# Causal attention on one core: TensorE takes the pieces of the weighted sum before a step's transposes

## The reference

```
q, k, v = x @ w_aq, x @ w_ak, x @ w_av         # 8 heads of 128
q, k = rope(q), rope(k)                        # rotary embedding
s = q k^T / 128, causal mask; p = softmax(s)   # 1024 x 1024 a head
r = sum over heads of (p v) @ w_ao
x = layernorm(x + r)
x = layernorm(x + ffn(x))                      # 128 -> 512 -> 512 -> 512 -> 128
```

## Time and profile before

| what | value |
|---|---|
| median of 3 runs | 1065.4 us (1064.43 to 1065.68) |
| profiled execution | 1065.99 us |
| its span, first to last instruction | 1064.2 us |
| attention stage, by the trace | from the start to about 773 us |
| mean granted TensorE clock | 0.981 of full speed |

### The profile page before, as it was taken

One profiled execution on the slowest core, in us unless ns is written; L12 is line 12 of the kernel. 1 busy time (PEld: TensorE's weight loads), 2 busy tenths in 40 slices (PEclk: granted clock), 3 DMA queues, 4 the chain that ended last, 5 costly groups with the idle time before them and its releaser, 6 DMA issues. The chain is left out here.

```text
span 1064.2 us, 19686 instructions
## 1 busy us (share of the span) xinstructions
PE 997.1 (94%) x5648; PEld 860.2 (81%) x5648; DVE 820.6 (77%) x1803; ACT 593.3 (56%) x1255; POOL 539.6 (51%) x536
## 2 busy tenths in 40 slices
PE   3799999999999999999999999999839999999995
PEld 3688888898888889888888888888728878788784
DVE  5888888888888888887888888788555677486744
ACT  3566666665666666566666666666434252433521
POOL 4666767776676776677677666767250101000000
PEclk9899999999999999999999999999969999999998
DMA  8433233432322123323222222221020000000000
GB/s 282 150 127 74 61 80 97 124 99 56 75 69 69 49 59 100 70 61 79 59 49 59 61 70 68 72 59 40 1 80 1 1 1 21 1 20 0 1 20 21
DMA packets 33292, 66.16 MB, mean 62 GB/s; under 512 B 5457, under 2 KB 6993, under 8 KB 32209
## 3 DMA queue, kind: packets, MB, share of 16 engines
q1 hardware_dynamic: 30400, 58.62, 21.0%
q10 hardware_dynamic: 2832, 6.82, 1.7%
HBM read 24.26 MB, written 7.34 MB: 30 GB/s over the span
## 5 line engine op out<-in xcount | busy, mean ns | idle before, releaser
L703 POOL TENSOR_SCALAR probs<-probs,inv_sum 128x128 f32<-128x128 f32 (+7 forms) x256 | 191.1, 747 | 232.4 <-DVE inv_sum L621 231.8
L534 ACT ACTIVATE pT<-psum 128x512 fp32r<-128x512 f32 (+3 forms) x384 | 173.9, 490 | 144.0 <-PE psum L401 141.9
L308 PE MATMUL psum<-pT,vals 128*128 128x512 f32 (+3 forms) x1152 | 242.6, 351 | 1.6 <-DVE rT L663 1.6
L522 ACT ACTIVATE probs<-psum,neg_max 128x128 f32<-128x128 f32 (+7 forms) x256 | 190.5, 744 | 80.2 <-DVE neg_max L615 79.8
L615 DVE TENSOR_REDUCE neg_max<-psum 128x1 f32<-128x128 f32 (+7 forms) x256 | 191.2, 747 | 54.8 <-PE psum L392 53.6
L631 DVE TENSOR_TENSOR pT<-psum,pT 128x512 fp32r<-128x512 f32 (+3 forms) x384 | 200.7, 551 | 32.3 <-ACT pT L534 25.3
L308 PEld LDWEIGHTS psum<-pT,vals 128*128 128x128 f32 x1152 | 187.7, 189 | 23.9 <-DVE pT L631 1.7
L401 PE MATMUL psum<-ident,probs 128*128 128x128 f32 x1152 | 173.7, 277 | 12.9 <-POOL probs L703 12.2
L883 PE MATMUL ps<-hid,w 128*128 128x512 f32 x768 | 181.3, 396 | 0.0
L708 POOL TENSOR_TENSOR swapped<-by_cos,swapped 128x512 f32<-128x512 f32 x128 | 164.7, 1298 | 14.2 <-DMA swapped<-by_sin 14.2
L883 PEld LDWEIGHTS ps<-hid,w 128*128 128x128 f32 x768 | 143.7, 188 | 34.5
(11 more groups left out here) (77 smaller groups left out, 1195.3 us busy)
## 6 DMA issues: line engine op xcount, KB each, us to landing
swapped<-by_sin SPq DMA_DIRECT2D x256, 128.0 KB, 2.3
w_stage<-qk_split SPq DMA_DIRECT2D x30, 256.0 KB, 2.7
wv_stage<-v_split SPq DMA_DIRECT2D x15, 256.0 KB, 2.7
x_split<-ffn_raw ACTq DMA_DIRECT2D x2, 1024.0 KB, 5.8
ffn_raw<-g SPq DMA_DIRECT2D x2, 1024.0 KB, 8.0
x_moving<-x_split SPq DMA_DIRECT2D x2, 1024.0 KB, 5.1
out<-y SPq DMA_DIRECT2D x4, 512.0 KB, 2.6
raw_x<-xT SPq DMA_DIRECT2D x3, 512.0 KB, 11.6
```

Of the source, the lines that this page charges most:

```text
L308: ins = nc.tensor.matmul(out_ap, left[a], right[b], start=first and i == 0, stop=last and i == 2)
L522: nc.scalar.activation(probs[:, ib % 4, :width].rearrange("p (h c) -> p h c", h=halves), score_ps[:, ib % 2, :halves, :half], ACT.Exp, bia ...
L534: nc.scalar.activation(pT[chunk][:, 0, 4 * f:4 * f + n_blocks, (ib % 4) * P:(ib % 4 + 1) * P], bank("t", head[1], nth)[:, :n_blocks * P].r ...
L703: nc.gpsimd.tensor_scalar(p, p, inv_sum[:, n:n + 1], 1.0, ALU.mult, ALU.mult).then_inc(probs_ready[0], 1)
```

## The change

In TensorE's step the two calls of `attend` move from the end of the step to the place between the scores and the transposes. No instruction is added or removed, each keeps its step, and the other engines' programs and the bank plan are the same.

```diff
--- before.py
+++ after.py
@@ -463,16 +463,16 @@
                     pe.wait_ge(vo_low, 1)
                 if exists(ahead):
                     scores(ahead, (s + 2) % NI)
+                if s in PV0_PIECES and exists(head):
+                    attend(head, 0, PV0_PIECES[s])
+                if s in PV1_PIECES and exists(step_on(head, -1)):
+                    attend(step_on(head, -1), 1, PV1_PIECES[s])
                 if exists(head):
                     transpose_probs(head, s)
                 for target, j in rope_tasks(head, s, QK_STEP):
                     project_qk(step_on(target, -1), j)
                 for c in v_tasks(head, s):
                     project_v(head[0], b, c)
-                if s in PV0_PIECES and exists(head):
-                    attend(head, 0, PV0_PIECES[s])
-                if s in PV1_PIECES and exists(step_on(head, -1)):
-                    attend(step_on(head, -1), 1, PV1_PIECES[s])
 
             run_pairs(pe, step)
```

## The result

The changed kernel takes 1119.1 us (median of 4 runs, 1118.2 to 1120.0) against 1065.3: a ratio of 1.0506, interval 1.0488 to 1.0524. The forecast was 1120. The span of the profiled execution is 1116.8 us against 1064.2.

What follows compares the result with a forecast made beforehand. TensorE was taken to set the pace, busy 997.1 of 1064.2 us. The three places, 10.2 + 28.2 + 16.5 = 54.9 us on 1066.0, gave 1120.9, as a median 1120.3; likeliest 1120, range 1080 to 1138.

Steps and rivals of the forecast that it cites:

- Place 1: Odd head, steps 3 to 6: late T(3) delays GpSimd's low part, S0' waits 1.5 us; net 0.68 a pair, 10.2 us.
- Place 2: Even head, step 6: A0's first piece waits for value 1's low part from VectorE, 1.79 us late; 28.2 us in sum.
- Place 3: T(7) into the next head: Q(0) of even heads and S(4) of odd heads wait, 1.1 us a pair, 16.5 us.
- What costs nothing: Later T(1), T(2), Q, V and moved A1 pieces are covered by other work; priced at zero.
- The seams: New orders of scores, pieces and transposes, some 160 seams: zero, with 0.05 us either way each, 8 us.
- The bank waits in step 5: Sign of being wrong: waits on banks in steps 2 to 5, which the prediction had priced at zero.
- the cover that I named: Steps 1 and 2: GpSimd takes swapped tile 2 only after block 5's normalization, 1.95 later; weights are used a head later.
- some 0.8 us of 46 can be won: Odd head, before T(6): TensorE's true loss is 0.82 us of a 46.13 us pair, the rest is full.
- rival B: Faster: the pieces cover the transposes' wait before T(6), 15 x 0.82 = -12, to 1053; chance 0.03.
- rival A: Only the value wait costs, 1.37 each; the odd head's 0.82 is won; +10, or 1075 to 1095; chance 0.20.
- Rival C: TensorE's clock falls to 1.2 GHz at each pair's 1.8 us stop, losing 56 us more, 1177; chance 0.03.
- windows with the clock below 1.00 inside the attention: Sign of being wrong, pointing to the clock rival; the forecast kept the granted clock at 1.00.

## Why the prediction was right, and where it was not

**Place 1**, 0.68 a pair: S0' 1.53 late, and 0.86 won between S0' and S1' (3.33 before, 2.47 after), 0.67 net. The chain came 1.86 later instead of 1.95; a release of 0.13 us behind L714 made up for it. S0''s delay is shown by the step-3 move alone, which makes all of it, and by its undoing, which leaves 0.56, what steps 1 and 2 make alone.

**Place 2**, 1.79 a pair: 1.79, of which 0.29 and not 0.42 is passed on by VectorE, and 0.13 is the release, which I had left out. I had also left out the 0.28 us in step 5, which the value wait covers. Undoing the wait gives back 1.60 us a pair; that its 28.2 us equal the term is luck.

**Place 3**, 1.10: 0.49 for Q(0) (0.44), 0.45 for S(4) (0.65), and 0.30 that I had not priced, in step 0 of the odd head: 1.24 in all. The shares of the last two differ from pair to pair, their sum does not. Step 7 alone costs 1.06, and there S(4) has 0.69.

**What costs nothing**: two errors that nearly cancel. The seams and covered steps were given as 0 with 8 us either way. The pair is 3.04 us longer and the places sum to 0.67 + 1.79 + 1.24 = 3.70, so all the rest was worth -0.66, or 10 us. From one scores group to the next, 0.25 of it is T(7) of the odd head, and 0.35 are steps 1, 2, 3 and 7 of the even head and 3 of the odd. The bank waits in step 5, named among the signs of being wrong, did appear. And steps 1 and 2 do delay the odd head's S0'; the cover that I named was not whole, and as the text said of its loss, it is place 1's chain that this delays.

**The step that failed** is the sentence that some 0.8 us of 46 can be won. The wait before T(6) was read as TensorE's alone. With step 6 moved alone it goes to T(7), which starts 8.16 us behind S(6) either way, and the time stays. In the whole change the 0.82 did come off, because S0' was late already. So the term was right here, and wrong as a statement about the kernel; rival B's 1053 and rival A's credit for it could not have been reached by covering T(6).

**The sum**: 54.9 us forecast, 52.6 in the profiled executions' spans and 53.8 in the medians. It is this near by cancellation too: 15 pairs gave 45.6 where the forecast's pairs gave 53.6; two longer pairs (3.5), the last pair (2.6, forecast at nothing) and the start (0.6) made up for much of it. Of these about 4.8 us are the lower clock, which the forecast excluded.

**Rival C**, the clock, was dismissed by a 1.62 us stop at full clock. Behind stops of 1.30, 1.42 and 2.26 us it did fall, at about 1.6 us each: three times in the attention, not in each of the 16 pairs, and not for 3.5. So the sign "windows with the clock below 1.00 inside the attention" appeared, at a twelfth of the rival's 56 us. The rule of the Trainium skill (TensorE: Matmul & The Clock Gate, "A second HAM failure mode: psum-queue depth-cycling") was right in kind; it gives no size.

## What to carry to other kernels

When a full engine's work is reordered, look at both ends: what the moved piece now waits for (here a value written 1.4 us too late, because one semaphore count stood for both key blocks), and what queues behind the piece it displaced (here one late transpose, two engines on, held up the next head's scores). An idle gap in front of one instruction is worth its length only if the next instruction of the same kind would not wait for the same engines; move the cover there first and see where the gap goes. Delays on one chain don't add, so undoing one part of a change shows less than its price, and doing it alone shows more.

## What the runs showed of the hardware

Behind a short stop in an otherwise full TensorE the granted clock fell in some cases and not in others, within one execution and between kernels. In the changed kernel it fell behind one of the 1.4 us stops before A0, which every pair from the second to the fifteenth has, and behind one of 15 stops before S0', the longest (1.30 us; the others 0.96 to 1.01). With step 7 behind the same first stop was 1.29 us long, and the clock stayed full. With step 3 alone ahead it fell twice behind the 1.00 us stop before S0', in the kernel with step 7 behind twice behind the 1.4 us stop, with only step 6 or only step 7 moved in no pair. The 2.26 us stop before the last A1 came with the lower clock in six kernels and without it with step 7 alone. Each such stretch inside a pair cost 1.5 to 1.6 us. What decides it was not tried.
